# Four-layer gated attention and mixture kernel: first norms half by half, router products behind the first tiles, routing in single steps, and more idle products

## What is computed

```python
x = x + jnp.tanh(g_xattn[0]) * _L0_xattn_ref(_layernorm(x, axis=-1), ctx_1024, ctx_1024, L0_xattn_Wu, L0_xattn_Wv)
x = x + jnp.tanh(g_ffn[0]) * _L0_ffn_ref(_layernorm(x, axis=-1), L0_ffn_gate_w, ...)   # softmax router, top 2 of 8
x = x + jnp.tanh(g_xattn[1]) * _L1_xattn_ref(...)                                      # 16 heads
x = x + jnp.tanh(g_ffn[1]) * _L1_ffn_ref(_layernorm(x, axis=-1), ...)                  # own norm, router, top 2 of 8
x = x + jnp.tanh(g_xattn[2]) * _L2_xattn_ref(...)                                      # linear, mean over the context
x = x + jnp.tanh(g_ffn[2]) * _L2_ffn_ref(...)                                          # 4-bit blocks, quantised
x = x + jnp.tanh(g_xattn[3]) * _L3_xattn_ref(...)
x = x + jnp.tanh(g_ffn[3]) * _L3_ffn_ref(...)                                          # router, top 2 of 8

# the routing of one mixture (layer 1)
probs = jax.nn.softmax(nx @ router_w, axis=-1)
_, idx = jax.lax.top_k(probs, K)
mask = jnp.sum(jax.nn.one_hot(idx, probs.shape[-1], dtype=probs.dtype), axis=1)
w = probs * mask
w = w / jnp.sum(w, axis=-1, keepdims=True)
```

## Time and profile before

| | us |
|---|---|
| three timed runs, median | 724.83 |
| lowest, highest | 722.32, 725.2 |
| profiled execution | 724.68 |
| its span | 722.9 |
| mean granted clock of TensorE | 0.964 of full |
| PE, DVE, ACT, POOL busy | 656.1, 479.8, 436.7, 182.7 |

### The profile page before, as it was taken

One profiled execution on the slowest core, in us unless ns is written; L12 is line 12 of the kernel. 1 busy time (PEld: TensorE's weight loads), 2 busy tenths in 40 slices (PEclk: granted clock), 3 DMA queues, 4 the chain that ended last, 5 costly groups with the idle time before them and its releaser, 6 DMA issues.

```text
span 722.9 us, 10213 instructions
## 1 busy us (share of the span) xinstructions
PE 656.1 (91%) x3563; PEld 478.1 (66%) x3573; DVE 479.8 (66%) x1093; ACT 436.7 (60%) x820; POOL 182.7 (25%) x215
## 2 busy tenths in 40 slices
PE   4889999998799799998999999997799997889997
PEld 1589996565466677776767667765555665667775
DVE  2477674587447567359657684368975763669996
ACT  4457454877436667668358486655127664877773
POOL 3414000541124033224241512041013001124531
PEclk9789999999789999999999999999999999999999
DMA  5112002020002000022010110010001000110001
GB/s 137 52 31 63 1 1 73 2 88 2 0 2 75 12 15 30 1 73 84 19 59 16 29 60 1 1 47 0 1 1 58 2 3 0 30 46 14 1 0 30
DMA packets 27361, 20.98 MB, mean 29 GB/s; under 512 B 5409, under 2 KB 22571, under 8 KB 27311
## 3 DMA queue, kind: packets, MB, share of 16 engines
q1 hardware_dynamic: 26591, 20.29, 9.3%
q10 hardware_dynamic: 720, 0.04, 0.1%
HBM read 19.80 MB, written 0.52 MB: 28 GB/s over the span
## 4 chain that ended last, share of the span: by engine, by line
PE 62%; DVE 17%; ACT 13%; issue 5%; POOL 2%; DMA 1%; ACTq 0%; DVEq 0%; POOLq 0%
PE PS L1483 54%; ACT PS L846 3%; PE PS L1723 2%; ACT H2h L843 2%; PE PS L1589 2%; ACT H1h L843 2%; ACT XN L753 1%; DVE ST L1020 1%; DVE H2l L1188 1%; DMA GW<-in_L_gate_T 1%; PE PS L1745 1%; PE PS L1504 1%; DVE ATT L1276 1%; ACT WH L737 1%; DVE H1l L1188 1%
## 5 line engine op out<-in xcount | busy, mean ns | idle before, releaser
L647 POOL TENSOR_TENSOR WL<-RAW,WH 128x512 fp32r<-128x512 f32 (+2 forms) x76 | 89.2, 1189 | 147.5 <-ACT WH L737 147.2
L1188 DVE TENSOR_TENSOR H2l<-PS,H2h 128x512 fp32r<-128x512 f32 x72 | 49.3, 689 | 57.9 <-ACT PS L846 57.4
L737 ACT ACTIVATE ATT<-PS 77x512 f32<-77x512 f32 (+5 forms) x92 | 46.7, 533 | 33.6 <-PE PS L1927 15.7
L639 POOL TENSOR_TENSOR RSTD<-VE,MHALF 128x4 f32<-128x4 f32 x18 | 18.6, 1032 | 185.1 <-DVE VE L1030 149.4
L1483 PE MATMUL PS<-XTh,WH 128*128 128x512 f32 x128 | 54.5, 426 | 11.0 <-DVE XTl L1048 4.1
L1483 PE MATMUL PS<-H1h,WH 128*128 128x512 f32 x146 | 60.2, 412 | 2.2 <-DVE H1l L1188 2.2
L665 POOL TENSOR_TENSOR XT<-XT,YW 128x512 f32<-128x512 f32 x24 | 32.2, 1342 | 113.1 <-DVE YW L1125 113.1
L1483 PE MATMUL PS<-H1l,WH 128*128 128x512 f32 x146 | 57.2, 392 | 0.0
L1483 PE MATMUL PS<-H1h,WL 128*128 128x512 f32 x146 | 57.1, 391 | 0.0
L1483 PE MATMUL PS<-XTl,WH 128*128 128x512 f32 x128 | 52.6, 411 | 0.0
L1483 PE MATMUL PS<-XTh,WL 128*128 128x512 f32 x128 | 52.6, 411 | 0.0
(11 more groups left out here) (254 smaller groups left out, 1651.0 us busy)
## 6 DMA issues: line engine op xcount, KB each, us to landing
RAW<-in_L_ffn_spec_W SPq DMA_DIRECT2D x4, 1024.0 KB, 5.5
RAW<-in_L_ffn_w SPq DMA_DIRECT2D x16, 256.0 KB, 3.0
RAW<-in_L_ffn_up_W SPq DMA_DIRECT2D x8, 256.0 KB, 2.7
RAW<-in_L_ffn_down_W SPq DMA_DIRECT2D x8, 256.0 KB, 3.4
RAW<-in_L_ffn_spec1a_W SPq DMA_DIRECT2D x2, 512.0 KB, 4.3
RAW<-in_L_ffn_spec1b_W SPq DMA_DIRECT2D x2, 512.0 KB, 5.6
RAW<-in_L_ffn_wg SPq DMA_DIRECT2D x4, 176.0 KB, 2.6
RAW<-in_L_ffn_wu SPq DMA_DIRECT2D x4, 176.0 KB, 2.7
```

The lines of the kernel that those rows point to most:

```text
L639: step(g.tensor_tensor(RSTD[:, c], VE[:, c], MHALF[:, c], ALU.pow))
L647: g.tensor_tensor(lo, RAW[0:r["rows"], r["raw"] + s["c0"]:r["raw"] + s["c1"]], hi.bitcast(fp32), ALU.subtract).then_inc(lo_done, 1)
L737: return s.activation(o, i, ACT.Copy)
L1188: v.tensor_tensor(lo, full, hi.bitcast(fp32), ALU.subtract).then_inc(split_done, 1)
```

## The change

It has six pieces.

1. Start: the first norm's scaling, turn and copies are done half by half, the first half ahead of the wait for the small loads and of the Wv product. Idle products are added: two before the scores, four before the turns of PB, one before the value products; the eight behind the value products become twelve.
2. Layer 0, first tiles: only the first half of the second norm stands before the mixture, with seven idle products behind its turn. The second half's turn (`x_last`) comes behind two tiles, the router products (`x_gate`) behind the third, the routing's first step before the fourth.
3. The routing is a list of single steps (`k` from 0 to 25) and `dealt` puts so many of them behind each item: two in layer 0 and in the first part of layer 1, one in the second part, two and then three in layer 3.
4. Layer 1: three `up` tiles come before `late_scale`, `late_stats` and `late_norm` behind the fourth; the router products (`scores`) are parted from the turn by one `spec0` tile; seven idle products stand before the last hidden part of the first `spec0` tile.
5. Before layer 2: seven idle products, the turn, context_part(1), two idle products, in place of context_part(1), four, the turn, four. In layer 2 the numbers 10, 6, 10, 18 become 12, 12, 14, 18.
6. Layer 3: the turn and the router products come before the weight strips, with six idle products between them, and the routing's first step opens the second group.

```diff
@@ -96,8 +96,19 @@
     def group(kind, layer, e, h, n, **more):
         return [piece(kind, layer, e, h, i, **more) for i in range(n)]
 
-    route = lambda: [dict(kind="route", part=k) for k in range(5)]
+    route = lambda layer: [dict(kind="route", k=k) for k in range(26)
+                           if not (layer == 0 and k >= 22 or layer == 3 and k in (2, 3))]
     second = [dict(kind="second")]
+    scores = [dict(kind="scores")]
+
+    def dealt(items, more, per):
+
+        out = []
+        for s in items:
+            out.append(s)
+            out += more[:per]
+            more = more[per:]
+        return out, more
...
         if n == 0:
-            k = route()
-            order[0] += k[0:1] + a[0:2] + k[1:2] + a[2:3] + k[2:3] + a[3:4] + k[3:4] + more
+            r = route(0)
+            order[0] += a[0:2] + chain("x_last") + a[2:3] + chain("x_gate") + r[0:1] + a[3:4] + more
         elif n == 1:
-            order[0] += a[0:1] + k[4:5] + weave(a[1:], b, c, more)
+            u = weave(a, b, c, more)
+            u, r = dealt(u, r[1:], 2)
+            order[0] += u + r
...
-    o += u[0:1] + chain("late_scale") + u[1:2] + chain("late_stats") + u[2:4] + chain("late_norm") + s[0:2] + second
+    o += u[0:3] + chain("late_scale") + u[3:4] + chain("late_stats", "late_norm") + s[0:2] + second + s[2:3] + scores
...
         if e % 4 == 0:
-            o += weave(s[2:] if e == 0 else spec("spec0", 0, TH), up(e, 1), new[:4])
-            k = route() if e == 0 else []
+            o += weave(s[3:] if e == 0 else spec("spec0", 0, TH), up(e, 1), new[:4])
+            k = route(1) if e == 0 else []
             o += k[0:1]
-            o += weave(spec("spec0", 1, TH), spec("turn", 0, 4, buf=2, hi="act"), new[4:], k[1:])
-            o += nxt[:1] + weave(spec("turn", 1, 4, buf=3, hi="act"), down(e, 0), nxt[1:2])
+            u, k = dealt(weave(spec("spec0", 1, TH), spec("turn", 0, 4, buf=2, hi="act"), new[4:]), k[1:], 2)
+            o += u
+            u, k = dealt(nxt[:1] + weave(spec("turn", 1, 4, buf=3, hi="act"), down(e, 0), nxt[1:2]), k, 1)
+            o += u + k
             o += weave(nxt[2:], down(e, 1))
...
-        order[3] += weave(a, {1: route()[1:3], 2: route()[3:]}.get(n, []), c, more)
         if n == 0:
-            order[3] += second + route()[0:1]
+            r = route(3)
+            order[3] += a + second + scores + more
+        elif n == 1:
+            order[3] += r[0:1] + a[0:2] + r[1:3] + a[2:3] + r[3:5] + a[3:4] + r[5:7]
+        elif n == 2:
+            a, r = dealt(weave(a, c, more), r[7:], 3)
+            order[3] += a + r
+        else:
+            order[3] += weave(a, c, more)
...
+                    if kind in ("split", "quantise", "scores", "down", "down0", "spec0", "spec1b", "weigh") or kind in HELD:
+                        if kind == "x_last":
+                            turned(1, split=True, halves=(1,), bank=PS[5])
...
                     if kind == "route":
-                        if s_["part"] == 0:
+                        if s_["k"] == 0:
...
+            scaled(0, 0, X, XN)
             act.wait_ge(in_first, 16 * len(FIRST))
             s.activation(TG[:, :], GB[:, :], ACT.Tanh).then_inc(tg_ready, 1)
-
+            scaled(0, 1, X, XN)
+            turned(0, halves=(0,))
             for i in range(2):
                 act.wait_ge(a0_up, i + 1)
                 copy(VP0[:, i * 4 * KC:(i + 1) * 4 * KC], PS[2 + i][0:R0, 0:4 * KC]).then_inc(a0_upc, 1)
-            for h in range(2):
-                scaled(0, h, X, XN)
-            turned(0)
+            turned(0, halves=(1,))
...
-            for h in range(2):
-                scaled(1, h, X, XN)
-            turned(1, split=True)
+            scaled(1, 0, X, XN)
+            turned(1, split=True, halves=(0,))
+            scaled(1, 1, X, XN)
...
+                third = lambda k: WGS[:, :, 32 * k:32 * k + E]
+                wg = WG[:, :].rearrange("p (t e) -> p t e", e=E)
+                if k == 0:
...
-                elif part == 1:
+                elif k == 1:
                     dve.wait_ge(gate_exp, n + 1)
                     if layer < 3:
 
                         now(v.tensor_reduce(RM[:, 1, :], rt3(1), AX.X, ALU.add))
-                        now(v.reciprocal(RM[:, 2, :], RM[:, 1, :]))
-                        now(v.tensor_tensor(rt3(2), rt3(1), per_token(RM, 2), ALU.mult))
-                elif part in (2, 3):
-
-                    pick = part - 2
+                elif k == 2:
+                    now(v.reciprocal(RM[:, 2, :], RM[:, 1, :]))
+                elif k == 3:
+                    now(v.tensor_tensor(rt3(2), rt3(1), per_token(RM, 2), ALU.mult))
+                elif k < 16:
+
+                    pick, m = divmod(k - 4, 7)
                     scores = 7 if pick else (9 if layer == 3 else 2)
...
+                    if m == 0:
+                        now(v.tensor_reduce(RM[:, 0, :], rt3(scores), AX.X, ALU.max))
...
+                    elif m == 5:
                         now(v.scalar_tensor_tensor(rt(7), rt(5), -1.0e30, rt(scores), ALU.mult, ALU.add))
-                else:
+                elif k == 16:
                     now(v.tensor_tensor(rt(8), rt(5), rt(6), ALU.add))
...
                     now(v.reciprocal(RM[:, 1, :], RM[:, 0, :]))
+                elif k == 20:
                     now(v.tensor_tensor(rt3(8), rt3(8), per_token(RM, 1), ALU.mult))
+                elif k == 21:
                     v.tensor_scalar(WG[:, :], rt(8), tg(4 + layer), None, ALU.mult).then_inc(wg_ready, 1)
...
+                elif k == 22:
+
+                    now(v.memset(WGS[:, :, :], 0.0))
+                    now(v.tensor_copy(third(0), wg))
+                elif k == 23:
+                    now(v.tensor_tensor(rt3(8), wg, third(0), ALU.subtract))
+                elif k == 24:
+                    now(v.tensor_copy(third(1), rt3(8)))
+                else:
+                    v.tensor_tensor(third(2), rt3(8), third(1), ALU.subtract).then_inc(wgs_ready, 1)
...
+                    elif kind == "x_last":
+                        low_of_xt(0, (1,))
...
-            low_of_xt(0)
+            low_of_xt(0, (0,))
...
-                            pe.wait_ge(xth_ready, first_xtl + RING[j - start] - 5)
+                            pe.wait_ge(xth_ready, first_xtl + 1)
...
+                        if kind == "x_last":
+                            turn(1, *normed(1, XN), halves=(1,), bank=PS[5])
+                        elif kind == "x_gate":
+                            logits(0, GW0[:, :], 1)
...
-                        k, src, w = (3, normed(4, XM), RW1) if layer == 1 else (7, normed(8, XN), RW3)
+                        k, src = (3, normed(4, XM)) if layer == 1 else (7, normed(8, XN))
                         turn(k, *src, halves=(1,), bank=PS[5])
+                        continue
+                    if kind == "scores":
+                        k, w = (3, RW1) if layer == 1 else (7, RW3)
+                        if layer == 3:
+                            keep_clock(6, PS[4])
                         logits(n, w[:, :], k)
                         continue
...
+                            if e == 0 and h == 0 and i == 0 and f == nf - 1:
+                                keep_clock(7, PS[4])
...
-            pe.wait_ge(in_first, 16 * len(FIRST))
             for i in range(2):
+                turn(0, *normed(0, XN), halves=(i,))
                 pe.wait_ge(ct_ready, i + 1)
+                if i == 0:
+                    pe.wait_ge(in_first, 16 * len(FIRST))
                 mm(PS[2 + i][0:R0, 0:4 * KC], Wv[:, :], CT[:, i * 4 * KC:(i + 1) * 4 * KC]).then_inc(a0_up, 1)
-            turn(0, *normed(0, XN))
             for i in range(2):
                 pe.wait_ge(xt_ready, i + 1)
                 mm(PS[i][0:R0, :], Wu[:, :], XT[:, i * HALF:(i + 1) * HALF]).then_inc(a0_up, 1)
+            pe.wait_ge(const_copied, 2)
+            pe.wait_ge(a0_upc, 2)
+            keep_clock(2, PS[2])
             pe.wait_ge(a0_upc, 4)
...
+            keep_clock(4, PS[2])
             for b in range(B):
...
+            keep_clock(1, PS[2])
             for b in range(B):
...
-            keep_clock(8)
-            turn(1, *normed(1, XN))
-            logits(0, GW0[:, :], 1)
+            keep_clock(12)
+            turn(1, *normed(1, XN), halves=(0,))
+            keep_clock(7)
             mixture(0, 0, 0)
...
             context_part(0)
+            keep_clock(7)
+            turn(4, *normed(5, XN), halves=(0,))
             context_part(1)
-            keep_clock(4)
-            turn(4, *normed(5, XN), halves=(0,))
-            keep_clock(4)
+            keep_clock(2)
             stream_part(0)
             keep_clock(6)
             turn(4, *normed(5, XN), halves=(1,))
...
-                keep_clock((10, 6, 10, 18)[p])
+                keep_clock((12, 12, 14, 18)[p])
```

40 lines of the change are left out of this document (16 added, 24 removed).

## The result

The changed kernel takes 716.75 us (median of four runs, 715.86 to 717.65), the kernel before 724.68 beside it (722.32 to 725.2): a ratio of 0.9903, 95% interval 0.9877 to 0.9928. It is faster by 8 us, where 18.4 had been forecast, and lies 0.75 us above the range. The profiled execution has a span of 715.8 and took 717.53.

What follows compares the result with a forecast made beforehand. PE, busy 91% of the span, was taken as the bound, with gains only where it idles or runs at the lower clock. Terms 3.4 + 6.9 + 4.2 + 0.4 + 3.5 = 18.4 us gave 706.3 from 724.7; range 701 to 716.

Steps and rivals of the forecast that it cites:

- Start of the kernel: Layer 0's first attention and mixture: earlier norms and first tiles, less DVE's routing and two table loads, gain 3.4 us.
- Rival (c): Layer 0's table loads cost twice the row's 1.28 us each: 2.6 us more, 708.9; chance 0.04.
- Layer 1, first tiles: Start of layer 1: shorter waits give 1.9 us, the clock staying up 5.0; sum 6.9 us.
- Rival (d): Layer 1's new order leaves the stall, last hidden part late and clock falling: 6.9 us lost, 713.2; chance 0.08.
- Layer 1, end of the routing: Routing dealt out in steps removes PE's 3.01 us wait and lower clock: 3.0 + 1.7 - 0.5 = 4.2 us.
- the 0.5 us for the scalings: Layer 1: scalings waiting for POOL's RSTD in DVE's queue make the turns 0.5 us later.
- Before and in layer 2: Joint before layer 2: +0.4 us from moved idle products; those among layer 2's four pairs fill waits, 0.
- Layer 3: Second half's tile starts 2 us sooner, WGS products no longer wait for routing, spread product 3.5 us earlier.
- Behind each place PE's dense stretch is only shifted.: Whole kernel: assumption under the 18.4 us sum that PE's dense work behind each gain just moves earlier.
- Rival (a): DVE binds more than assumed in layer 0, layer 1's routing and layer 3: gain 11.9 us, 712.8; chance 0.24.
- Rival (b): Clock up from layer 0's value products (2.4 us), no fall behind layer 1's router products (1.7): 702.2; chance 0.18.
- Rival (e): 44 added idle products, uncovered at the lower clock, cost 18.9 us: 725.2 or above; chance 0.04.

Runs made afterwards that it cites:

- again: The changed kernel, unaltered, profiled once more: 716.30 us.
- l0_alone: The kernel before with only the change's layer 0 parts: 723.30 us, ratio 0.9989.
- all_covers: The changed kernel with the idle products of covers, scalings passed by route items, layer 3's early weighing and eight idle products before layer 2's weight turns: 705.10 us.
- held_old_l0: all_covers with layer 0 put back to the old order up to the end of its mixture: 711.66 us.
- covers: The changed kernel with idle products meant for eight of PE's waits, never more than the wait is long: 713.32 us, ratio 0.9822.
- l1_start: The kernel before with only the change's new start of layer 1, its seven idle products included: 718.52 us, ratio 0.9916.
- before_held: The kernel before, in its own order and without any part of the change, with idle products in PE's waits: 717.58 us, ratio 0.9909.
- scales: The changed kernel with layer 1's scalings on VectorE passed by the route items, no longer right behind the next route step: 714.69 us, ratio 0.9847.
- l3_alone: The kernel before with only the change's layer 3 part: 723.14 us, ratio 0.9990.

## Why the prediction was right or wrong

**Start of the kernel: 3.4 forecast.** Nearly every station is near: the last U0T copy at 16.4 (forecast near 17), the first tile at 31.53 (33), two table loads at 36.37 and 38.68 (near 39), the ninth tile on DVE at 52.5 (52.0 to 53.7). Only the second norm's turn came 3 us before its forecast, at 27.87 for 30.9, and the clock, up from 22.6, fell again at 29.5. DVE gives back most of the 7.8 us head start, as forecast: at the ninth tile 3.1 are left. The end of the mixture gains 1.5 us in the changed kernel's profile, behind its fall at 53.4, 2.8 in `again`, 2.9 in l0_alone and 4.4 where the clock stays up (all_covers against held_old_l0). So the term was right up to the ninth tile, and was 0.8 us in the kernel's time when alone.

The Trainium skill ("ScalarE: Activation LUTs", What ACT_TABLE_LOAD costs) adds a drain of 1.38 us to each load. This case disagrees: the pair cost the chain 1.4 us in all, and the Silu at 39.98 follows the load that began at 38.68 without a gap. Rival (c) is out.

**Layer 1, first tiles: 6.9 forecast, 6.4 measured alone.** Right in the sum, wrong in its halves (order 4.5, idle products 1.9, for 1.9 and 5.0). Rival (d) is out. The clock fell behind the router products at 200.2, as assumed; in covers and all_covers it did not.

The Trainium skill ("TensorE: Matmul & The Clock Gate", HAM oscillation — how this bites in real kernels) makes idle gaps the cause of falls. Most falls here do stand behind a wait of PE, and idle products in the waits removed most of them; but the same 2.0 us wait had a fall in one kernel and none in another, so had the 1.93 us wait that was never filled, and the fall at 200.2 has no wait over 0.2 us in the 10 us ahead of it.

**Layer 1, end of the routing: 4.2 forecast, 1.9 at the WGS products, 0.7 alone.** The 1.9 is from the router products to the WGS products, 41.0 us for 42.9 in l1_start. The 3.01 us wait went with its fall. The step that failed is the 0.5 us for the scalings: the turns came 1.4 us late, PE stood 2.50 us instead of 1.09 and the clock fell there. Mended and held, the dealing is worth 3.4 to 4.3 us. The WGS products came 7.9 us sooner, not the 14 of the forecast (3.4 + 6.9 + 4.2).

**Before and in layer 2: 0.4 forecast.** 0.3 in the trace, and nothing in layer 2, as put.

**Layer 3: 3.5 forecast.** The second half's first tile came 8.29 us behind the layer's first, for 10.25 before: 2.0, as put. The spread products gained 2.5 instead of 3.5, because DVE's steps still held the WGS products (1.18 us of idle). The step that failed is "the WGS products no longer wait for the routing", and the weighing behind them was missing from the sum altogether: it was late next.

**The sentence that lost most, by the traces,** is the one below the sum: "Behind each place PE's dense stretch is only shifted." A shifted stretch meets its own short waits at other moments. One stretch at 53.4, two at 176.3, one at 227.5, one at 329.9 and the second one behind 630.2 are six that the kernel before doesn't have, at up to 1.7 us each: at most 10 of the 10.4 us that were missing. How much of it is shown: idle products in those waits and a few older ones gave 3.7 us by the medians, 9 in the profiled executions. The two order edits on DVE gave 2.3 and 2.5, in part through falls that went with the waits, so the two causes can't be priced apart. Against them two that it had in and before layer 2 are gone, where DVE sets the pace. The rest of the miss is DVE's, the scalings and the weighing. Rival (a) had 6.5 of the 10.4, from DVE alone. Rival (b), a clock better than assumed, failed at both its places: the clock was up at the value products but fell again at 29.5, and it fell behind the router products of layer 1. It was better only where nobody had put it, behind the router products of layer 3. `all_covers` took 705.1 us, below the forecast of 706.3, but that does not make the forecast right: it has idle products that also hold the clock at old waits, and against `before_held` it gains 12. Rival (e), slower by idle products, was the opposite of what they do: `covers` adds 65 more and is 4 us faster.

## What to carry to other kernels

A gain on PE's path can be given back at the next wait behind which the clock falls: before summing terms, list every wait of 1 us or more behind the change, and fill those with idle products in the bank that the waiting product will write, counted at the full clock and kept below the wait. Then look in the trace whether they ran in that wait; here six of them stood one set of turns too early. Put them into the kernel before as well, or their gain is taken for the change's. Time each part of a change once alone and once taken out of a version in which the later waits are held; the two differed by 5 us for layer 0 and by 3.6 for the dealing. When a wait goes, look at what stands next in the releasing engine's queue behind something not yet ready.

## What the runs showed of the hardware

Waits of 1.05 to 2.5 us on PE were followed by a lower clock for 3.4 or 6.8 us in some kernels and by none in others, with the same code and the same length of wait (2.01 us with a fall at 329.9 in the changed kernel, 2.03 without one at 327.77 in scales); two executions of one kernel agreed on most places. Router products, 16 of 8 columns, were followed by a fall at 200.2 (changed kernel) and 601.0 (covers) with no wait over 0.7 us ahead, and by none in layer 1 of covers. With eight idle products of 1.8 us in an unrelated place, two stretches some 108 us later were gone, and the median shows no cost. The record of the granted clock does not hold at the kernel's start: in l3_alone seven idle products take 3.19 us, the time of the lower level as in the earlier trace rows, in a window that gives 1.00:

```profile
30.36 3.19 PE L1527 MATMUL PS<-MB,identb 128*128 128x512 bf16 x7 [0.22 <-issue]
...
20.00:32.00 12.00, 10.96 (x44) 9.28 (x46) 6.50 (x24) 2.26 (x5) 4.52 (x5) 1.00 0.14 38
```

There the products' lengths have to be read instead.
